# A perceiver layer on one core: one program from the query block to the scores, the heads' content stored by single tiles, more zero products, and the first weight step's rounding later

## The reference, cut to what matters

```python
# context attention
Q = einsum('btx,dx->btd', layernorm(x), Wq) + bq
K = einsum('bpx,dx->bpd', ctx, Wk) + bk
x = x + einsum('btp,bpd->btd', softmax(Q K^T / 32), ctx)
# latent attention, y = layernorm(x)
c_q, c_kv = y @ Wq_down, y @ Wkv_down
q_c = c_q @ Wq_up;   k_c = c_kv @ Wk_up;   v_c = c_kv @ Wv_up
q_r = y @ Wq_rope;   k_r = y @ Wk_rope                 # k_r is shared by all heads
scores = (q_c k_c^T + q_r k_r^T) / sqrt(72)
x = x + (softmax(scores) @ v_c) @ Wo
# FFN, twice: linear8bit(x, W, b)
outlier = max|x| by column > 3
x_in, x_out = where(outlier, 0, x), where(outlier, x, 0)
y = quant_rows(x_in) @ quant_rows(W).T + x_out @ W.T + b
```

## Time and profile before

| | |
|---|---|
| runs shown | 923.29, 924.41, 924.37 us, median 924.37 |
| profiled execution | 925.35 us, of which the span is 923.3 |
| mean granted TensorE clock | 0.994 |
| busy | PE 895.4, DVE 684.6, ACT 627.3, POOL 488.9 us |
| DMA | 174.82 MB, 189 GB/s over the span |

### The profile page before, as it was taken

The page is one execution under the profiler, slowest core; times in us unless marked ns, Lnnn a source line. Parts: engine busy times, 40 slices in busy tenths (PEclk is TensorE's granted clock), DMA queues, the critical chain, the costliest instruction groups (busy, mean ns, idle before and its releaser), DMA issues.

```text
span 923.3 us, 19052 instructions
## 1 busy us (share of the span) xinstructions
PE 895.4 (97%) x6866; PEld 818.6 (89%) x6866; DVE 684.6 (74%) x1090; ACT 627.3 (68%) x1093; POOL 488.9 (53%) x334
## 2 busy tenths in 40 slices
PE   8999999999999899999999999999899999999997
PEld 6997888888887789999999999987689999899997
DVE  6447676768456468888888888996888888887754
ACT  5424444465444568888888888986678787878762
POOL 0220000045443797777778777773176676376673
PEclk9999999999999999999999999999999999999999
DMA  8566756678754779566565655556232433224221
GB/s 327 190 206 237 293 207 273 249 267 318 275 202 147 221 228 307 174 195 193 179 190 177 213 176 190 176 192 199 93 137 97 178 128 145 92 93 164 109 92 46
DMA packets 80696, 174.82 MB, mean 189 GB/s; under 512 B 7632, under 2 KB 57584, under 8 KB 78064
## 3 DMA queue, kind: packets, MB, share of 16 engines
q1 hardware_dynamic: 79920, 173.63, 53.8%
q10 hardware_dynamic: 704, 0.23, 0.1%
HBM read 161.51 MB, written 11.53 MB: 187 GB/s over the span
## 4 chain that ended last, share of the span: by engine, by line
PE 73%; DVE 6%; ACT 4%; POOL 3%; issue 2%; DMA 2%; SPq 0%; DVEq 0%; ACTq 0%; POOLq 0%
PE bank L51 17%; PE bank L53 17%; PE bank L52 17%; PE bank L1408 4%; PE bank L1409 3%; PE bank L549 3%; PE bank L1379 3%; PE bank L1804 2%; PE bank L2089 2%; PE bank L1424 2%; POOL W_all L2328 1%; DMA ring<-in_L_attn_Wq_rope_dram 1%; POOL wl L1003 1%; PE bank L1391 1%; PE bank L731 1%
## 5 line engine op out<-in xcount | busy, mean ns | idle before, releaser
L1003 POOL TENSOR_TENSOR wl<-ring,wh 128x1024 fp32r<-128x1024 f32 x68 | 161.9, 2402 | 0.0
L51 PE MATMUL bank<-act_all,W_all 128*128 128x256 f32 (+1 forms) x512 | 154.0, 301 | 2.3 <-POOL W_all L2328 1.9
L51 PE MATMUL bank<-act_all,wh 128*128 128x256 f32 x512 | 144.5, 282 | 1.3 <-DVE qq L1609 0.9
L52 PE MATMUL bank<-act_all,wh 128*128 128x256 f32 x512 | 144.1, 281 | 0.0
L53 PE MATMUL bank<-act_all,W_all 128*128 128x256 f32 (+1 forms) x512 | 144.0, 281 | 0.0
L53 PE MATMUL bank<-act_all,wl 128*128 128x256 f32 x512 | 143.8, 281 | 0.0
L513 POOL TENSOR_TENSOR xa_WT_l<-ring,xa_WT_h 128x1024 fp32r<-128x1024 f32 x16 | 43.4, 2732 | 176.6 <-ACT xa_WT_h L508 166.7
L2328 POOL TENSOR_TENSOR W_all<-rnd,W_all 128x512 fp32r<-128x512 f32 x72 | 92.3, 1292 | 57.4 <-ACT W_all L2215 52.1
L1616 DVE TENSOR_TENSOR pl<-bank,ph 128x512 f16<-128x512 f32 x128 | 88.1, 688 | 44.4 <-ACT ph L1555 41.6
L1000 POOL CAST wh<-ring 128x1024 fp32r<-128x1024 f32 x68 | 68.8, 1041 | 69.5 <-PE bank L53 62.2
L51 PEld LDWEIGHTS bank<-act_all,W_all 128*128 128x128 f32 x512 | 97.1, 190 | 3.4 <-POOL W_all L2328 2.5
(11 more groups left out here) (275 smaller groups left out, 2604.2 us busy)
## 6 DMA issues: line engine op xcount, KB each, us to landing
ring<-in_ctx_dram SPq DMA_DIRECT2D x16, 2048.0 KB, 8.1
ring<-in_L_attn_Wq_rope_dram SPq DMA_DIRECT2D x32, 1024.0 KB, 6.4
ring<-in_L_ffn_W_dram SPq DMA_DIRECT2D x14, 2048.0 KB, 7.7
panel<-in_L_ffn_W_dram SPq DMA_DIRECT2D x48, 512.0 KB, 4.6
w1p<-in_L_ffn_W_dram SPq DMA_DIRECT2D x16, 512.0 KB, 3.7
ring<-in_L_xattn_Wq_dram SPq DMA_DIRECT2D x2, 2048.0 KB, 12.5
ring<-in_L_xattn_Wk_dram SPq DMA_DIRECT2D x2, 2048.0 KB, 7.8
ring<-in_L_attn_Wo_dram SPq DMA_DIRECT2D x4, 1024.0 KB, 5.0
```

The lines of the kernel that those rows point to most:

```text
L51: pe.matmul(out, lh, rh, start=start, stop=False, skip_group_check=True)
L52: pe.matmul(out, lh, rl, start=False, stop=False, skip_group_check=True)
L1003: pool.tensor_tensor(half_of(l, i), half_of(r, i), f32(half_of(h, i)), ALU.subtract).then_inc(w_lo, 1)
```

## The change

Four things are changed.

**One program from the query block to the scores.** The functions `query_*` are called first in the block that was the second; there is no block end between. The `qrow` transposes move ahead of the products i = 0 to 3 of c = 1, and the first four tiles of context chunk 0 are turned (`turn_context`) ahead of the products i = 4 to 7 of c = 1, with ACT's and DVE's parts for them between those for the products. The scores begin with tiles 4 to 7. SP loads chunk 1 after panels 4 and 5 rather than after 4 to 7, and DVE takes the maxima of panels 6 and 7 after the parts of tiles 4 to 7.

**Content by single tiles.** SP spreads `krope` to the first four heads alone, stores tile 0 of q and k (six DMAs of 128 KB), waits for that spread, loads content(0), and only then issues the other two spreads, the six stores of tile 1 (counted by `stored_left`, waited for at g = 4) and `next_w(2)`. ACT's table load for exp moves from before the `krope` copies to behind the value copies.

**Zero products:** 8 for 3, 10 for 6, and 7 for 5 at three places. **Rounding:** in the FFN's first weight step DVE rounds tiles (0, 1), 2, 3 at k = 5, 6, 7 rather than 4, 5, 6, and ACT's `biased` for tile 0 comes at k = 6, for 1 to 3 at k = 7, rather than (0, 1) at 4, 2 at 5, 3 at 6.

```diff
@@ query block
-                            for q in range(4, IN_Q):
+                        for q in (4, 5):
                                 load_panel(sp, q, q % 2, w1_n[q])
...
-                        if not c:
-                            for q in (2, 3):
+                    for q in (2 + 4 * c, 3 + 4 * c):
                                 load_panel(sp, q, q % 2, w1_n[q])
...
+                def turn_context(k):
+                    if k == 0:
+                        landed(pe, 0, USE_SCORES)
+                    for j in range(CH):
+                        last = pe.transpose(bank[k][:, j * P:(j + 1) * P], raw(0)[:, j, k * P:(k + 1) * P], ident[:, :])
+                    last.then_inc(sb_ready, 1)
...
+                        if (i0, c) == (0, 1):
+                            pe.wait_ge(a_misc, 2)
+                            for t in range(QT):
+                                last = pe.transpose(bank[1][:, t:t + 1], qrow[:, t * P:(t + 1) * P], ident[0:1, 0:1])
+                            last.then_inc(qbk_ready, 1)
                             for i in range(i0, i0 + 4):
+                            if i0 and c:
+                                pe.wait_ge(a_misc, 3)
+                                turn_context(i - i0)
...
+                    if i >= 4:
+                        act.wait_ge(sb_ready, i - 3)
+                        act.activation(WT_h[0][:, i - 4, :], bank[i - 4][:, :], ACT.Copy).then_inc(sb_hi, 1)
...
@@ scores
-                for k in range(KT):
-                    if k >= 4:
+                for k in range(4, KT):
                         pe.wait_ge(sb_lo, k - 3)
                     turn(0, k)
+                pe.wait_ge(ob_lo, 2 * KT)
...
-                for k in range(KT):
+                for k in range(4, KT):
                     low(0, k, k + 1)
+                for q in range(6, IN_Q):
+                    maximum_panel(dve, q % 2, q // 2, am1[:, q:q + 1])
@@ content
-                    for b in range(QBUF):
-                        sp.dma_start(f32(kmix[0:ROPE, b * GROUP:(b + 1) * GROUP, :]),
-                                     f32(krope[0:ROPE, 1, :]).unsqueeze(1).to_broadcast([ROPE, GROUP, T])).then_inc(k_spread, 16)
+                    spread_keys(sp, 0)
                     for i in range(2):
-                        store_content(sp, 0, i)
-                    sp.wait_ge(k_spread, QBUF * 16)
+                        sp.wait_ge(con_lo, i + 1)
+                        store_tiles(sp, i, slice(0, 1), stored[0])
...
@@ heads
+                        elif g == 4:
+                            sp.wait_ge(stored_left, 2 * SLOTS * 16)
...
-                    next_w(2)
+                    sp.wait_ge(k_spread, 16)
+                    sp.wait_ge(cleared, 2 * QBUF + 1)
                     for g in range(FIRST, NG):
...
                             content(g + 2)
+                        if g == FIRST:
+                            for b in (1, 2):
+                                spread_keys(sp, b)
+                            for i in range(2):
+                                store_tiles(sp, i, slice(1, 2), stored_left)
+                            next_w(2)
+                            sp.wait_ge(k_spread, QBUF * 16)
@@ FFN
-            TILES_AT_FIRST = ((), (), (), (), (0, 1), (2,), (3,), ())
+            TILES_AT_FIRST = ((), (), (), (), (), (0, 1), (2,), (3,))
+            BIASED_AT_FIRST = ((), (), (), (), (), (), (0,), (1, 2, 3))
...
-                        keep_warm(pe, 4, 3)
+                        keep_warm(pe, 4, 8)
...
-                        keep_warm(pe, 2, 6)
+                        keep_warm(pe, 2, 10)
...
-                        keep_warm(pe, 2, 5)
+                        keep_warm(pe, 2, 7)
```

More of the change, by code:

```diff
@@ new lines, in query_sync @@
+            def query_sync(sp):
+                for h in range(2):
+                    sp.dma_start(xr[:, 0, COLS[h]], x_t[:, 0, COLS[h]]).then_inc(in_x[h], 16)
+                sp.dma_start(xr[:, 1, :], x_t[:, 1, :]).then_inc(in_x[2], 16)
+                for c in range(2):
+                    load(sp, c, raw(c), wq_t[:, CH * c:CH * c + CH, :])
+                for c in range(2):
+                    sp.wait_ge(tb_ready, YT + KT * (c + 1))
+                    load(sp, c, raw(c), wk_t[:, CH * c:CH * c + CH, :])
+                    load_panel(sp, c, c, w1_n[c])
+                for c in range(2):
+                    if c:
+                        for q in (4, 5):
+                            load_panel(sp, q, q % 2, w1_n[q])
+                    sp.wait_ge(wk_dve, 2 * (c + 1))
+                    sp.wait_ge(wk_pool, 2 * (c + 1))
+                    load(sp, c, raw(c), ctx_t[c])
+                    for q in (2 + 4 * c, 3 + 4 * c):
+                        load_panel(sp, q, q % 2, w1_n[q])
@@ new lines, in query_gpsimd @@
+            def query_gpsimd(pool):
+                pool.memset(ident[:, :], 0.0).then_inc(consts, 1)
+                pool.memset(f32(zero[:, :]), 0.0).then_inc(consts, 1)
+                pool.wait_ge(consts, 2)
+                pool.affine_select(out=ident[:, :], in_=ident[:, :], compare_op=ALU.not_equal, fill=1.0,
+                                   base=0, pattern=[[-1, P]], channel_multiplier=1).then_inc(consts, 1)
+                for c in range(2):
+                    for j in (2, 3):
+                        pool.wait_ge(wk_hi, CH * c + j + 1)
+                        pool.tensor_tensor(nat_l(c)[:, j, :], raw(c)[:, j, :], f32(nat_h(c)[:, j, :]),
+                                           ALU.subtract).then_inc(wk_pool, 1)
@@ new lines, in main_q @@
+            def main_q(pe, c, jj):
+                v = CH * c + jj
+                if v >= 4:
+                    pe.wait_ge(ob_lo, v - 3)
+                for k in range(KT):
+                    pe.wait_ge(tb_lo, YT + KT * c + k + 1)
+                    last = product(pe, bank[4 + v % 4][:, 0:T],
+                                   (WT_h[c][:, k, jj * P:(jj + 1) * P], WT_l[c][:, k, jj * P:(jj + 1) * P]),
+                                   (act_h[0][:, k, :], act_l[0][:, k, :]), k == 0, k == KT - 1)
+                last.then_inc(ob_ready, 1)
@@ L603, in step @@
                             scores_out(c, b, k // 4)
-                for k in range(KT):
+                for k in range(4, KT):
                     high(0, k, k + 1)
+                act.wait_ge(a_misc, 3)
                 with act.Fori(0, NCTX // 2 - 1) as i:
@@ L2309, in _ @@
                     w2_rows = lambda b: lambda j: rw2[:, CH * b + j:CH * b + j + 1]
-                    step(0, 0, None, None, first=True, tiles=TILES_AT_FIRST)
+                    step(0, 0, None, None, first=True, tiles=BIASED_AT_FIRST)
                     with act.Fori(0, NW1 // 2 - 2) as i:
```

377 lines of the change are left out of this document (172 added, 205 removed).

## The result

The changed kernel took 926.09 us (median of 22 executions), the kernel before 923.90 in the same job (22); the ratio is 1.002, 95% interval 1.0013 to 1.0027. By the ratio it is slower by 1.9 us, where 1.75 faster was forecast. In a later job it was 1.0021 (1.0009 to 1.0034).

What follows compares the result with a forecast made beforehand. TensorE, busy 895.4 of 923.3 us, was taken as the bound, with its waits and low-clock stretches as targets. Terms -1.9 + 3.5 - 0.9 - 2.45 = -1.75 gave 922.6 against the median; range 918.0 to 926.5.

Steps and rivals of the forecast that it cites:

- rival 4: Heads: rope weight of g = 2 lands as slowly as g = 3's, 12.3 us; time 927.0; chance 0.12.
- A: Query block to scores: joining the blocks removes idle and speeds transposes, less a late context chunk 2; -1.9 us, bounds -3.1 and -0.4.
- B: Heads' content: rope weight lands 1.75 us later and the clock falls for 1.75; +3.5 us, bounds -1.6 and +7.9.
- C: FFN's rows: added zero products fill idle before 652 and hold the clock; -0.9 us, bounds -1.0 and +0.3.
- D: FFN's first weight step: rounding in a row saves 0.75 idle and a 1.7 clock fall; -2.45 us, bounds -2.6 and -0.5.
- The sum's guess of 0.11 per transpose: Scores' start: 36 transposes at 0.11 us each, between 0.141 and 0.09, make the stretch 4.2 us, a gain of 2.35.
- The fall of the clock for another 1.75: Heads: after 4.2 us idle at w3 the clock falls to half for some 3.5 us, costing 1.75.
- Rival 2: Heads: rope weight of g = 2 lands in 6.4 us or less, no clock fall; time 918.3; chance 0.25.

Runs made afterwards that it cites:

- a_alone: The kernel before with only the first part, one program from the query block to the scores: 923.00 us, ratio 0.9979.
- acd: The changed kernel with the content by single tiles undone and the table load in its old place: 921.83 us, ratio 0.9963; repeated at 921.20, 0.9961.
- ab: The changed kernel with the FFN's part (zero products and rounding) undone: 926.10 us, ratio 1.0016 to the kernel before.
- acd_table: acd with the exp table load moved behind the value copies, as in the change: 920.55 us, ratio 0.9964 to the kernel before.
- d_alone: The kernel before with only the rounding and bias of the FFN's first weight step moved: 923.61 us, ratio 0.9987.
- b_again: Second run of the kernel before with only the content by single tiles and the table load moved: 928.87 us, ratio 1.0035.
- the three reordered kernels: The changed kernel with g = 2's rope weight behind content(0), 1.0017; ahead of content(0), 0.9991; ahead, with tile 1's stores behind content(1), 0.9998.

## Why the prediction was wrong

**The forecast was 922.6, -1.75; measured +1.9.** The 926.09 us lie inside the stated range of 918.0 to 926.5, but that is luck: this end of the range was rival 4's, a landing time of 12.3, which did not happen. By term, in us:

| term | forecast | alone | in the changed kernel |
|---|---|---|---|
| A, one program | -1.9 | -1.9 | -0.7 and -2.0, by the profile of before; -1.0 against the usual 243.3 |
| B, content | +3.5 | +3.1, +3.2 | +3.3 and +3.1 in stages 288 to 617; 5.5 by the ratios |
| C + D, FFN | -3.35 | -1.5 | -2.45 in stages 648 to 795; nothing measurable behind B by the ratios |

**Right:** what A is worth, by its own steps. The idle at the border went; context chunk 2 was issued at 79.76 (80.4 said) and TensorE waited 0.77 and 0.62 for it (0 to 0.75 said), 0.68 in a_alone. The sum's guess of 0.11 per transpose was near: 20 take 2.42 us from start to start of what follows, 0.12 each, and the scores' first product stands at 75.37 (75.7 said). In the changed kernel 0.25 and 0.48 more were lost at 216, for a DVE part; this wait stands in no profile of acd, and its cause is not known.

**Right in kind, and in size by offsetting errors:** B. TensorE's own gains (kmix, the table load) were waited away at w3 and POOL's chain behind the rope weight set the time. But the six stores of tile 1 took 5.3 us to issue, not 2.5 to 3; against the forecast's 313.6, shifted as far as the other stages are, the weight was issued at 316.14. It landed in 6.95, not 7.9, at 323.09. With the 1.19 us by which all stands earlier at 288 this is 3.3 later than the 320.95 of before, where +1.75 was forecast. The fall of the clock for another 1.75 was not there in the first profile (1.00 over 322 to 348). The second has a fall, 0.63 over 332 to 336, and yet its stage is 0.36 shorter; its wait at w3 is shorter instead, in PE's timeline:

```profile
341.83 0.39 PE L51 MATMUL bank<-act_all,wh 128*128 128x256 f32 x1 [1.07 <-POOL wl L1020]
```

The same holds for ab: with the content part the stage is 316.68 and 316.85 in the two profiles with a fall in the heads, and 316.97 to 317.04 in the four without. While TensorE waits for POOL's chain anyway, work at half clock in between costs nothing in these profiles: the term for the clock should have been zero, and that for the late weight 3.3. Two waits were missing in the forecast, 1.99 for w2 and 1.52 for content(1). As POOL's chain ends last, they took from the wait at w3 (2.76 for the 4.2 said) rather than adding to it. The rival on a landing time of 12.3 did not happen. Rival 2 asked for a landing within 6.4 us (320.95 - 314.8 is 6.15, strictly), and the six profiles with the weight behind tile 1's stores have 6.8 to 7.6. The Trainium skill's fit, "DMA: Bandwidth & Descriptors", "Anatomy of one DMA", which is for a DMA over GpSimd, would give as an estimate some 4.4 us for this load. Here it took 6.95 with other transfers in flight, and the shortest of all 1 MB loads in this trace 4.8, so this case does not bear the estimate out.

**Wrong:** C and D. The step of the prediction that failed is that the sum priced the two clock falls at their full length, as they stand in one profile: 0.9 in C and 1.7 in D. Both falls are in it, and in the second one. But those two executions took 925.35 and 927.13, above their medians of 924.37 and 924.8, and the mean clock of 132 executions of before is 0.9963, where a profile with both falls has 0.994 and profiles without any fall have 0.998 to 0.999. So an average execution has about one fall of the two, in one place or another, and half of the 2.45 us was to be had: 1.5 measured. The times say the same. Of the 144 executions of before whose clock is on record, the 14 with a mean of 0.999 took 923.76 us on average and the 28 with 0.994 took 926.00. These 2.2 us are near the 2.45 of both falls, and most executions lie between.

D was too large where both falls do stand, too: 1.6 in the profiles, not 2.45. The fall cost 1.2 (1.7 said), and the rounding itself brought 0.4 (0.75 said), since TensorE now waits 0.61 for ACT's rows at 702. The sign was there in the table of times ahead of the prediction: the profiled execution was 1.0 above the median, and I used this as an offset of all terms rather than as a reason to discount two of them.

**The second step that failed** is that the terms were simply added. The parts measured alone come to -1.9 + 3.1 - 1.5 = -0.3. That accounts for 1.45 of the 3.65 us between forecast and result; the other 2.2, a little more than the intervals of the ratios together allow, appear only where the parts stand together, and their cause stays open. What the record says of it:

- Profiles of the changed kernel against an execution of before without falls: A -0.7 to -1.0, B +3.3, C 0, D -0.4, together +1.9 to +2.2, and measured were +1.9 and +1.9. That fits, but an average execution of before has a fall, and then 1 us of it is missing.
- Against the two profiles of acd (spans 919.6 and 919.3) the changed kernel's 923.1 and 924.5 are 4.4 longer. The stages 288 to 617 have 3.6 of it, and 45 to 288 has 1.1, where the content part changes nothing.
- The clock is a small part. The mean clock is 0.9962 in the changed kernel and 0.9975 and 0.9985 in acd. The changed kernel's eleven executions with 0.995 took 926.96 on average, its thirteen with 0.997 and above 925.97, which is still 4.3 above acd's mean of 921.66.

Why the FFN's part gives less behind the content part is not settled either; the two or three profiles of each are too few.

**The versions that beat both:** adt (first part, rounding, table load) 0.9952 with 920.89 us, and acd_table 0.9964 with 920.55. They are the changed kernel without its content part (adt without the zero products too), 5 to 6 us faster than it. Their intervals overlap with that of acd.

## To carry to other kernels

A stretch at a lower clock in one profile is worth its length only as often as it comes; compare the mean clock and the time of the profiled execution with those of the others before it is put into a sum. Where a chain of another engine sets the time, as POOL's did here, neither TensorE's gains nor its losses in between counted, its clock among them: only the moment counted at which that chain was fed. Terms that were each measured alone need not add up; the sum has to be measured as a sum. And where many DMAs are issued by one engine, splitting a store to get one load earlier moved the next load back here: the six stores took 5.3 us to issue, and in the three reordered kernels a waiting SP held up all behind it for 3.3 to 7.4 us.

## What I had not expected of the hardware

- The same idle (0.5 and 1.65 us within 6 us) was followed by a granted clock of 0.5 in both profiles of one kernel and by 1.00 in four profiles of others (a_alone, d_alone, b_again, adt).
- The same issues take longer where others stand close ahead: three stores of 128 KB took 1.30 us from SP's queue when nothing had been issued for 3.4 us (304.41 to 305.71 in the changed kernel) and 2.94 right behind two loads and two spreads.
- The first 45 us varied by 1.7 us between executions (44.70 to 46.41 in 20 profiles of kernels that are alike there), nearly as much as the whole change is worth.
